# Routed experts on tokens sorted by expert, with the router moved into the batch loop

## The chip, the cores and the metric

One NeuronCore of a Trainium2 chip runs the whole program. The metric is device time in microseconds for one execution. Before the change three runs took 994.24, 994.62 and 994.80 us; the median is 994.62 us.

## What is computed

A pre-norm decoder layer on x of 16 batches x 256 tokens x 128 channels, in float32:

```
x = x + attention(layernorm(x))          # 16 heads of 8 channels, masked scores
x = x + cross_attention(layernorm(x))    # 1601 context rows per batch
x = x + ffn(layernorm(x))

ffn: scores  = softmax(x @ gate_w.T)                  # 8 experts
     indices = top_k(scores + gate_bias, 2)
     combine = one_hot(indices) * scores, summed over the 2 choices
     y = sum over e of mlp(x, w1[e], w2[e], w3[e]) * combine[:, e]
     z = mlp(x, sw1, sw2, sw3)                        # the shared expert
     mlp(x) = (silu(x @ w1.T) * (x @ w3.T)) @ w2.T    # 128 -> 256 -> 128
```

So each of the 4,096 tokens needs two of the eight experts, and the shared one.

## The kernel before

The kernel is written engine by engine: each engine has its own list of instructions in an order written out by hand, and semaphores join them. The activations stay in SBUF in `xall` (32 tiles of 128 tokens).

**The batch loop.** `batches` (L455 on) calls `step(i, nxt, new, old, crs)` on every engine for i = -1 to 17. A step works on four batches at once: it prepares batch i+1 (`nxt`: first layernorm, q and k, their split into bfloat16 parts that go through HBM and come back as `kst` and `qst`), runs the self attention of batch i (`new`: `alpha` with the row maxima, `gamma`, `p_exp`, `masked`, `values`), finishes self attention of batch i-1 (`old`: L717, L1020 to L1024, L750, L759, second layernorm, q of the cross attention and its low part `q2_lo`, L1096), and runs the cross attention of batch i-2 (`crs`: four units of `cross_scores`, `cross_max`, `cross_exp`, `cross_transposes`, `cross_values`, then L1091 adds the result to `xall`). Steps 2 to 14 are one hardware loop.

What sets the order around the change:

- TensorE (`step` from L555): `alpha(0, 1)`, then `cross_scores(0)`, which waits for `q2_lo_done` of VectorE; the matmul that makes v (L709); `alpha(1, 3)`, where `alpha(u)` waits for the row maximum of `alpha(u-2)`; L717; the sums over v (L723 to L725), which wait for `v_done`; `alpha(3, 4)` (L581); `cross_transposes(0)`; and so on to `values(3)`.
- VectorE (`step` from L943): `alpha_max(0, 1)`, `statistics` of batch i+1 (L959, L962), v (L1006), `cross_max(0)` (L984), `alpha_max(1, 2)`, den, num and rden; at the end of the step `heads_out(0)` (L1078, after the second `values`), the four adds of L1091, `q2_lo` (L1096), `heads_out(1)`.
- GpSimd: `inverse_deviation` (L1114, L1116), `on` (L1153), the two subtractions L1159 and L1161, later `info_low` (L1131: 896 and then 512 columns), `masked` (L1142), `xb` (L1206).
- SyncE issues all DMAs.

**The FFN.** `shared_step` is called with g = -4 to 7. It prepares group g+4 (4 tiles, 512 tokens: layernorm, transposes, the split of the transposed tokens into `x3_hi` and `x3_lo`, router logits) and runs the shared expert of group g. Its calls with g = -4 to -1 lie in the last step of the batch loop (`beside`), the others behind it in `rest`. A token group and one expert are one unit: `up` is 12 matmuls of 512 columns (L194: w13_hi x x_hi, w13_lo x x_hi, w13_hi x x_lo, for four blocks), Silu on ScalarE (L268), the product on VectorE (L306), `down` is 8 float32 matmuls of 128 x 128, each of which the profile shows as two (L203). The routed pass runs 8 groups x 8 experts = 64 such units, every token through every expert; VectorE adds each result into `xall`, scaled by the token's weight for that expert (L395). Router arithmetic is done once, on 128 x 256 (L324 to L347).

Of the kernel before, what the change touches and what calls it, by code (L numbers as in the profile page):

```python
# [11 lines left out]
BF16 = mybir.dt.bfloat16  # L12

# [27 lines left out]
NEG = -1.0e30  # L41
QROWS = 48
# [3 lines left out]
C_ID, C_MASK, C_U, C_ONE, C_CNT, C_BV, C_BR, C_BIAS, C_GB, C_IOTA, C_END = 0, 128, 256, 384, 512, 544, 672, 800, 804, 812, 820  # L46


def decoder_kernel(nc, x, ctx, ctxT, consts, wq, wk, wv, wr, wx, gate, w13, w2, out):
    with ExitStack() as stack:  # L50
# [10 lines left out]
        dk = nc.dram_tensor("k_stack", [HA, 6, P // HA, S], BF16).ap()  # L61

# [87 lines left out]
        def flat(b0, n):  # L150
# [4 lines left out]
        xn3, xn3T = sb("xn3", [P, GT, D]), sb("xn3T", [P, GN])  # L155
        Y_BANKS = (4, 7)
        x3_hi, x3_lo = sb("x3_hi", [P, NT * P], F32R), sb("x3_lo", [P, NT * P], F32R)
        st3, mv3, rstd3 = sb("st3", [P, GT, 6]), sb("mv3", [P, GT, 2]), sb("rstd3", [P, 2, GT])
        logit, ex, sc, biased, eq, oh1, oh2, comb = (sb(n, [P, NT, E]) for n in
                                                     ("logit", "ex", "sc", "biased", "eq", "oh1", "oh2", "comb"))  # L160
        lmax, esum, erec, m1, i1, m2, i2 = (sb(n, [P, NT]) for n in ("lmax", "esum", "erec", "m1", "i1", "m2", "i2"))
        comb_g = sb("comb_g", [P, GT, E])
        sil = [prob[z][:, 2 * GN:3 * GN] for z in range(2)]
        h = [[prob[n][:, z * GN:(z + 1) * GN] for z in range(2)] for n in range(2)]
        for n in ("ln3_stats", "ln3_aggr", "ln3_eps", "ln3_rstd", "xn3_done", "xn3T_ps", "xn3T_sb", "x3_lo_done", "lg_ps", "lg_sb",
                  "route", "ex_done", "comb_done", "comb_g_done",
                  "up_ps", "silu_done", "h_done", "y_ps", "shared_done", "acc_done"):
            s[n] = sem(n)

        def shared_step(step, g):

            step(g, g < NGR - 4, -3 <= g < NGR - 3, -2 <= g < NGR - 2, g >= 0)

        def routed_pass(eng, group):  # L180
            group(0, False)
            with eng.Fori(1, NGR) as g:
                group(g, True)

        def moe_pe(pe):
            def up(u, g, e, first=False):

                for z in range(2):
                    if not first:
                        pe.wait_ge(s["h_done"], 2 * u - 1 + z)  # L190
                    for half_w in range(2):
                        w = slice(half_w * INTER + z * P, half_w * INTER + (z + 1) * P)
                        for n, (a, b) in enumerate(((w13_hi, x3_hi), (w13_lo, x3_hi), (w13_hi, x3_lo))):
                            mm = pe.matmul(ps[:, 2 * z + half_w, :], lhsT=a[:, e, w], rhs=b[:, bass.ds(g * GN, GN)],  # L194
                                           start=(n == 0), stop=(n == 2))
                    mm.then_inc(s["up_ps"], 1)

            def down(u, e, n):

                pe.wait_ge(s["h_done"], 2 * u + 2)  # L200
                for t in range(GT):
                    for z in range(2):
                        mm = pe.matmul(ps[:, Y_BANKS[n], t * D:(t + 1) * D], lhsT=h[n][z][:, t * P:(t + 1) * P], rhs=w2_sb[:, e, z, :],  # L203
                                       start=(z == 0), stop=(z == 1))
                mm.then_inc(s["y_ps"], 1)

            def step(g, stats, norm, trans, new):
                f = g + 2
                if trans:
                    pe.wait_ge(s["xn3_done"], GT * f + GT)  # L210
                    if f:
                        pe.wait_ge(s["xn3T_sb"], 2 * f)
                    for t in range(GT):
                        mm = pe.transpose(ps[:, 5, t * P:(t + 1) * P], xn3[:, t, :], ident)
                    mm.then_inc(s["xn3T_ps"], 1)
                if new:
                    pe.wait_ge(s["x3_lo_done"], g + 1)
                    up(g, g, E, g == 0)
# [1046 lines left out]
```

## Time and profile before

| | |
|---|---|
| median of three runs | 994.62 us |
| the profiled execution: its span | 997.1 us (2.5 us over the median; no other time of it is given) |
| instructions | 19,846 |
| PE busy | 896.1 us, 90% of the span |
| DVE busy | 540.2 us, 54% |
| ACT busy | 425.3 us, 43% |
| POOL busy | 289.7 us, 29% |
| DMA | 57.49 MB, mean 58 GB/s |
| share of L194 (up) and L203 (down) in the chain that ended last | 20% and 13% |

The span has three parts. Up to about 620 us the batch loop runs, with a period of 36.0 us from step 2 on; then come the last step of the loop with the preparation of the FFN beside it, and the shared expert up to about 692 us; the rest is the routed pass. Times in the profile count from the span's start. A busy PE is not a PE at its peak, and an engine's idle time costs something only where the next engine waits for it.

### The profile page before, as it was taken

The page shows a single profiled execution, that of the slowest core. Times are in us where ns is not written, and L with a number is a line of the kernel's source. Part 1 is how long each engine was busy: PE and PEld are TensorE (multiplying, and loading weights), DVE is VectorE, ACT ScalarE, POOL GpSimd, SP SyncE. Part 2 cuts the span into 40 slices and gives each one's busy share as a digit, 9 for nine tenths or more (in the row PEclk, how much of TensorE's full clock was granted, in tenths as well). Part 3 has the DMA queues.
Part 4 walks back from the last instruction along what each step waited for, and adds up shares of the span by engine and source line. Part 5 has one row for each costly group of instructions (what it writes and reads, how often), then busy time and mean ns, then how long its engine had stood idle before and what let it go on. Part 6 is the DMA issues. An engine that isn't in the chain of part 4 may idle for free.

```text
span 997.1 us, 19846 instructions
## 1 busy us (share of the span) xinstructions
PE 896.1 (90%) x6528; PEld 694.8 (70%) x6528; DVE 540.2 (54%) x1291; ACT 425.3 (43%) x887; POOL 289.7 (29%) x495
## 2 busy tenths in 40 slices
PE   1697998998898899899899887789999999999998
PEld 0354766666676676676666666779888888888887
DVE  0443565475475465556547543556655555555554
ACT  1133555545645645555554564334222222222221
POOL 2235345435435524634633543242000000000000
PEclk9995999999999999999999999789999999999999
DMA  7124144134134224414413411000000000000000
GB/s 237 32 51 105 42 112 128 34 99 123 40 99 116 58 82 116 93 52 111 126 34 101 124 36 58 9 1 1 2 11 1 11 11 0 11 11 0 11 11 11
DMA packets 64282, 57.49 MB, mean 58 GB/s; under 512 B 5872, under 2 KB 57984, under 8 KB 64128
## 3 DMA queue, kind: packets, MB, share of 16 engines
q1 hardware_dynamic: 64256, 57.15, 21.8%
q8 instruction: 15, 0.25, 0.1%
q14 instruction: 11, 0.09, 0.0%
HBM read 45.20 MB, written 11.53 MB: 57 GB/s over the span
## 4 chain that ended last, share of the span: by engine, by line
PE 77%; ACT 5%; issue 5%; DVE 5%; POOL 3%; SPq 1%; DMA 1%; POOLq 0%; DVEq 0%; ACTq 0%
PE banks L194 20%; PE banks L203 13%; PE banks L653 7%; PE banks L610 7%; PE banks L588 4%; PE banks L636 4%; PE banks L590 3%; PE banks L691 3%; POOL prob L1142 3%; PE banks L581 2%; PE banks L583 2%; ACT prob L862 2%; DVE xmax L984 2%; PE banks L717 1%; PE banks L672 1%
## 5 line engine op out<-in xcount | busy, mean ns | idle before, releaser
L268 ACT ACTIVATE prob<-banks 128x512 f32<-128x512 f32 x144 | 86.0, 598 | 228.1 <-PE banks L194 178.7
L306 DVE TENSOR_TENSOR prob<-banks,prob 128x512 f32<-128x512 f32 x144 | 99.3, 691 | 107.0 <-ACT prob L268 106.9
L203 PEld LDWEIGHTS banks<-w_sb,prob 128*128 128x128 f32 x1152 | 139.1, 192 | 6.0
L203 PE MATMUL banks<-w_sb,prob 128*128 128x128 f32 x1152 | 140.4, 275 | 0.0
L194 PE MATMUL banks<-x_hi,w_hi 128*128 (+1 forms) x288 | 120.7, 419 | 0.1
L653 PE MATMUL banks<-info,xprobT 128*128 128x128 f32 (+1 forms) x832 | 108.3, 282 | 9.6 <-ACT xprobT L838 9.6
L976 DVE TENSOR_REDUCE mx<-banks 128x2 f32<-128x512 f32 x128 | 87.3, 683 | 50.8 <-PE banks L590 50.7
L194 PE MATMUL banks<-x_lo,w_hi 128*128 (+1 forms) x288 | 114.3, 397 | 0.0
L862 ACT ACTIVATE prob<-banks 128x512 f32<-128x512 f32 x192 | 99.8, 617 | 32.4 <-PE banks L676 32.4
L194 PE MATMUL banks<-x_hi,w_lo 128*128 (+1 forms) x288 | 113.6, 394 | 0.0
L653 PEld LDWEIGHTS banks<-info,xprobT 128*128 128x128 f32 (+1 forms) x832 | 100.0, 195 | 17.2 <-ACT xprobT L838 17.2
L826 ACT ACTIVATE xprob<-banks,xmax 128x896 f32<-128x896 f32 x64 | 59.3, 927 | 122.6 <-DVE xmax L984 122.6
L1142 POOL TENSOR_SCALAR_AFFINE_SELECT prob<-prob 128x256 f32<-128x256 f32 (+1 forms) x192 | 87.8, 482 | 34.8 <-ACT prob L862 34.5
L395 DVE SCALAR_TENSOR_TENSOR xall<-banks,comb_g,xall 128x128 f32 (+1 forms) x256 | 72.1, 344 | 34.9 <-PE banks L203 34.9
L984 DVE TENSOR_REDUCE xmax<-banks 128x1 f32<-128x896 f32 x64 | 62.5, 977 | 28.5 <-PE banks L610 19.3
L636 PE MATMUL banks<-cst,xprob 128*128 128x128 f32 (+1 forms) x416 | 58.1, 279 | 20.5 <-ACT xprob L826 20.5
L838 ACT COPY xprobT<-banks 128x512 f32<-128x512 f32 (+2 forms) x128 | 58.6, 509 | 33.6 <-PE banks L636 31.5
L636 PEld LDWEIGHTS banks<-cst,xprob 128*128 128x128 f32 (+1 forms) x416 | 48.1, 143 | 25.6 <-ACT xprob L826 24.1
L194 PEld LDWEIGHTS banks<-x_lo,w_hi 128*128 128x128 f32 x288 | 54.3, 189 | 13.4
L194 PEld LDWEIGHTS banks<-x_hi,w_lo 128*128 128x128 f32 x288 | 54.7, 190 | 10.1
L972 DVE TENSOR_REDUCE mx<-banks 128x4 f32<-128x512 f32 x64 | 43.7, 683 | 32.9 <-PE banks L583 32.8
L194 PEld LDWEIGHTS banks<-x_hi,w_hi 128*128 128x128 f32 x288 | 54.6, 190 | 9.9 <-DVE prob L306 0.3
(143 smaller groups left out, 1388.3 us busy)
## 6 DMA issues: line engine op xcount, KB each, us to landing
infoT<-in_ctxT SPq DMA_DIRECT2D x16, 800.5 KB, 5.8
info<-in_ctx SPq DMA_DIRECT2D x16, 768.0 KB
kst<-k_stack SPq DMA_DIRECT2D x32, 192.0 KB
q_parts<-parts SPq DMA_DIRECT2D x32, 96.0 KB, 2.3
k_stack<-parts SPq DMA_DIRECT2D x32, 96.0 KB, 2.3
qst<-q_parts SPq DMA_DIRECT2D x32, 96.0 KB
w_raw<-in_w SPq DMA_DIRECT2D x16, 144.0 KB, 5.5
k_stack<-parts SPq DMA_DIRECT2D x32, 64.0 KB, 2.1
```

The costliest lines, as they stand in the source:

```text
L194: mm = pe.matmul(ps[:, 2 * z + half_w, :], lhsT=a[:, e, w], rhs=b[:, bass.ds(g * GN, GN)], start=(n == 0), stop=(n == 2))
L203: mm = pe.matmul(ps[:, Y_BANKS[n], t * D:(t + 1) * D], lhsT=h[n][z][:, t * P:(t + 1) * P], rhs=w2_sb[:, e, z, :], start=(z == 0), stop=(z ...
L268: act.activation(sil[z], ps[:, 2 * z, :], ACT.Silu).then_inc(s["silu_done"], 1)
L306: dve.tensor_tensor(h[n][z], ps[:, 2 * z + 1, :], sil[z], ALU.mult).then_inc(s["h_done"], 1)
L395: dve.scalar_tensor_tensor(xt, ps[:, Y_BANKS[e % 2], t * D:(t + 1) * D].unsqueeze(1), comb_g[:, t, e:e + 1], xt, ALU.mult, ALU.add).then_i ...
L610: mm = pe.matmul(ps[:, c, 0:m1 - m0], lhsT=a[:, q], rhs=b[:, m0:m1], start=(n == 0), stop=(n == 2))
L636: mm = pe.transpose(ps[0:w, 3 + z, (m - part[0]) * P:(m - part[0] + 1) * P], xprob[hf][:, o:o + w], ident)
L653: mm = pe.matmul(ps[:, 2, u * P:(u + 1) * P], lhsT=xprobT[hf][0:w, m - blocks[0], :], rhs=info[0:w, m, :], start=(m == blocks[0]), stop=(m ...
L862: act.activation(prob[n % 2][:, kind * 512:(kind + 1) * 512], ps[:, KEY_BANKS[v % 4], :], ACT.Exp, scale=SCALE).then_inc(s["p_exp"], 1)
L976: dve.tensor_reduce(mx[:, 1, h:h + 2], bank.rearrange("p (c n) -> p c n", c=2), AX.X, ALU.max).then_inc(s["alpha_max"], 1)
L984: dve.tensor_reduce(xmax[:, u:u + 1], flat(0, HW[hf]), AX.X, ALU.max, negate=True).then_inc(s["xmax_done"], 1)
L1142: pool.affine_select(out=v, in_=v, compare_op=ALU.is_gt, fill=0.0, base=0, pattern=[[0, 4 if kind == 2 else 2], [1, P]], channel_multiplier=-1
```

## The change

`step` gets two more stages. With `rte`, batch l = i-3 is normalised, transposed and split, and its logits and its two choices are computed; with `pos`, batch o = i-4 gets the places of its rows, and the rows are sent. The loop now has steps -1 to 19, of which 4 to 14 are the hardware loop. Tokens sorted by expert lie in HBM: `sorted_rows` has a region of 4,224 rows for each expert, and a row is the 128 normalised channels, the token's weight and the row number that its result goes to (520 bytes). Each token is sent twice, by four indirect DMAs of 128 rows per batch, issued by GpSimd. Behind the loop VectorE works out the expert and the first row of each of 72 tiles (64 full ones' worth, up to 8 for the experts' rests; all 72 are always run). The FFN is then: shared groups 0 to 3; 36 pairs of sorted tiles; shared groups 4 to 7; the sum.

The core of the diff, per engine:

```diff
+TOPK = 2
+PAIRS = (B * S * TOPK // P + E) // 2
+SLOTS = 2 * PAIRS
+SB = 4
+EARLY = NGR // 2
...
-                step(-1, True, False, False, False)
...
-                with eng.Fori(2, B - 1) as i:
-                    step(i, True, True, True, True)
...
+                with eng.Fori(4, B - 1) as i:
+                    step(i, True, True, True, True, True, True)
...
+                step(B + 2, False, False, False, False, True, True)
+                step(B + 3, False, False, False, False, False, True)
```

TensorE, in a step and behind the loop:

```diff
                 cross_scores(0)
                 if old:
                     pe.wait_ge(s["oT_sb"], 2 * j + 2)
+                if pos:
+                    pe.wait_ge(s["picked"], o + 1)
+                    pe.wait_ge(s["tri_done"], 2)
+                    first = oh_bf[:, 0, :].unsqueeze(1)
+                    pe.matmul(ps[:, 7, 0:2 * E], lhsT=tri_bf[:], rhs=oh_bf[:].rearrange("p t e -> p (t e)"),
...
+                    pe.matmul(ps[:, 7, 2 * E:3 * E], lhsT=ones_bf[:], rhs=oh_bf[:, 1, :],
+                              start=False, stop=True, skip_group_check=True).then_inc(s["rank_ps"], 1)
                 if new:
...
                 cross_scores(1)
+                if rte:
+                    pe.wait_ge(s["xn3_done"], 2 * l + 2)
+                    for t in range(T):
+                        mm = pe.transpose(ps[:, 7, S + t * P:S + (t + 1) * P], xn3[:, t, :], ident)
...
                 cross_scores(3)
+                if rte:
+                    for t in range(T):
+                        mm = pe.matmul(ps[:, 7, S + t * E:S + (t + 1) * E], lhsT=xn3T[:, t * P:(t + 1) * P], rhs=gate_sb[:],
+                                       start=True, stop=True)
...
+            def experts_of(q):
+                for j in (2 * q, 2 * q + 1):
+                    expert[j] = pe.value_load(expert_i[0:1, j:j + 1], min_val=0, max_val=E)
+            def sorted_up(q):
+                for t in range(2):
+                    of = bass.ds(expert[2 * q + t], 1)
+                    for n, (a, b) in enumerate(((xT_hi, w13_hi), (xT_lo, w13_hi), (xT_hi, w13_lo))):
+                        mm = pe.matmul(ps[:, UP_BANKS[q % 2] + t, :], lhsT=a[g % 2][:, c], rhs=b[:, of, :].rearrange("p o n -> p (o n)"),
+                                       start=(n == 0), stop=(n == 2))
...
+                for g in range(EARLY):
+                    up(g)
+                    if g:
+                        down(g - 1)
+                down(EARLY - 1)
+                pe.wait_ge(s["slots_done"], 1)
+                experts_of(0)
+                sorted_x(0)
+                pe.wait_ge(s["shared_done"], EARLY)
+                for q in range(PAIRS):
+                    if q + 1 < PAIRS:
+                        experts_of(q + 1)
+                    sorted_up(q)
+                    if q % 2 == 0 and q // 2 + 1 < PAIRS // 2:
+                        sorted_x(q // 2 + 1)
+                    if q >= 1:
+                        sorted_hT(q - 1)
+                    if q >= 2:
+                        sorted_down(q - 2)
```

`sorted_x` transposes 4 tiles of sorted rows, `sorted_hT` is 4 transposes of the hidden values of a pair, `sorted_down` 4 float32 matmuls. ScalarE copies and splits (`sorted_hi`, `sorted_T`), does Silu (`sorted_silu`) and scales each tile's result by the row's weight (`sorted_y`, two per pair); VectorE does `sorted_lo` and `sorted_hid`.

VectorE in a step:

```diff
+                places()
                 alpha_max(0, 1)
+                if rte:
+                    apart(dve, "x3_done", 4 * l + 4)
+                    statistics(l, st3, mv3, "ln3_stats", "ln3_aggr")
                 if nxt:
...
                 alpha_max(2, 3)
+                if rte:
+                    normalised(l, mv3, rstd3, xn3, "ln3_rstd", "xn3_done")
...
+                route_scores()
                 heads_out(0)
+                route_choices()
                 if crs:
...
                 heads_out(1)
```

In the part left out of the last lines stand the four adds of L1091 and `q2_lo` (L1096), unchanged. `places` is 5 instructions, the first of which waits for `rank_ps`; `route_scores` is 2; `route_choices` is a chain of 18 on 128 x 16 or 128 x 32, nearly each of which waits for the one before it. Eleven of the 18 have two tensors in SBUF as inputs. In TensorE's part, the three rank matmuls have 8 to 16 columns in bfloat16.

ScalarE in a step: the copies of the transposed tokens and of the logits, the cast to `x3_hi`, and the exponential of the scores behind `p_exp(1)`.

GpSimd in a step: `inverse_deviation` of batch l at its head; the four indirect DMAs ahead of `on`; `x3_lo`, the copy of the normalised tokens into `row` (twice) and of the home numbers behind `info_low(1, ...)`, ahead of `xb`. Behind the loop 72 indirect DMAs (`sorted_home`), one for each tile's result into `routed_out`:

```diff
+                if pos:
+                    apart(pool, "placed", o + 1)
...
+                    for t in range(T):
+                        for c in range(TOPK):
+                            pool.indirect_dma_start(dsort, bass.IndirectOffsetOnAxis(ap=place[:, t, c:c + 1], axis=0), row[:, c, t, :], None,
+                                                    bounds_check=SORTED - 1, oob_is_err=False).then_inc(s["sent"], 16)
...
+                for j in range(SLOTS):
+                    sorted_home(j)
```

SyncE behind the loop: 8 register loads with two DMAs each (the pads behind each expert's rows), a wait for all rows sent, then for each of the 72 tiles a register load and a DMA of 128 rows into one of four buffers of 4 tiles (from the fifth group on after the results of the group four earlier have landed), then, once all results have landed, 16 DMAs of 256 KB that bring the two routed results of each token back. VectorE adds them to `xall` in 16 instructions of 128 x 512, and SyncE writes the output in 8 DMAs as before.

Removed: the 64 units of the routed pass, the 256 scaled adds (L395), the router arithmetic behind the loop, and the calls of `shared_step` in the last step of the loop (`beside`).

## Rows read from the trace of the kernel before

**Rows 1.** Stretches: batch loop and routed pass. us, then busy PE, PEld, DVE, ACT, POOL, clock, DMA share, GB/s
```profile
168.00:564.00 396.00, 360.74 (x3036) 259.15 (x3033) 230.01 (x518) 222.35 (x495) 182.84 (x320) 1.00 0.34 89
706.00:999.00 293.00, 286.81 (x1756) 252.49 (x1754) 160.05 (x389) 74.09 (x124) 0.00 (x0) 0.99 0.02 7
```

**Rows 2.** Chain that ended last, one unit of the routed pass: start us, us, what
```profile
977.35 2.80 PE banks L194 x12
980.15 1.78 PE banks L203 x16
```

**Rows 3.** Timeline, tail of batch step 13: start us, us, engine line op
```profile
524.63 0.69 DVE L1078 COPY oT<-banks 128x512 f32<-128x512 f32 x1 [2.11 <-PE banks L694]
...
525.77 1.38 POOL L1142 TENSOR_SCALAR_AFFINE_SELECT prob<-prob 128x512 f32<-128x512 f32 x3
...
525.98 1.25 DVE L1091 SCALAR_TENSOR_TENSOR xall<-banks,xw,xall 128x128 f32 x4 [0.66 <-POOL xw L1199]
...
527.12 1.27 POOL L1131 TENSOR_TENSOR info_lo<-infoT,info_hi 128x512 fp32r<-128x512 f32 x1
...
527.34 1.34 DVE L1096 TENSOR_TENSOR q_lo<-q,q_hi 128x256 fp32r<-128x256 f32 x1
```

**Rows 4.** Timeline, head of batch step 13
```profile
492.80 0.19 PEld L610 LDWEIGHTS banks<-info_hi,q_hi 128*128 128x128 f32 x1 [0.40 <-POOL info_lo L1131]
...
493.78 0.47 DVE L959 BATCH_NORM_STATS2 st<-xall 128x6 f32 x2
...
494.12 0.61 PE L709 MATMUL banks<-wv_sb,xn1T 128*128 128x128 f32 x4
...
494.76 0.42 DVE L1006 TENSOR_TENSOR vaug<-banks,cst 128x256 f32<-128x256 f32 x1
...
495.10 1.08 DVE L984 TENSOR_REDUCE xmax<-banks 128x1 f32<-128x896 f32 x1
...
495.63 1.04 PE L717 MATMUL banks<-cst,oT 128*128 128x128 f32 x8
...
497.27 0.39 PE L581 MATMUL banks<-kst,qst 48*128 48x128 bf16 x4
...
500.47 0.39 PE L588 MATMUL banks<-kst,qst 48*128 48x256 bf16 x2
```

**Rows 5.** All q_lo instructions (L1096): ns min/median/max, first and last start us
```profile
L1096 DVE TENSOR_TENSOR q_lo<-q,q_hi x16: 425/1336/1341, 93.7 to 620.9; 128x256 fp32r<-128x256 f32 x16
```

**Rows 6.** Timeline, DVE: a very small instruction, and two dependent ones of the router
```profile
515.44 0.16 DVE L1067 TENSOR_TENSOR xmin<-xmax 128x2 f32<-128x2 f32 x1
...
694.30 0.43 DVE L330 TENSOR_TENSOR sc<-ex,erec 128x256 f32<-128x256 f32 x1
694.76 0.42 DVE L331 TENSOR_TENSOR biased<-sc,cst 128x256 f32<-128x256 f32 x1
```

**Rows 7.** Stretches in the last batch step, as in rows 1
```profile
622.00:624.00 2.00, 0.91 (x5) 0.55 (x3) 1.05 (x2) 0.00 (x0) 0.00 (x0) 0.82 1.00 294
624.00:626.00 2.00, 0.77 (x4) 0.78 (x5) 1.20 (x9) 1.10 (x2) 0.38 (x2) 0.50 0.02 4
```

**Rows 8.** Timeline, first matmul of the shared expert
```profile
651.77 0.78 PE L194 MATMUL banks<-x_hi,w_hi 128*128 128x512 f32 x1
```

**Rows 9.** DMA: an issue on SyncE's queue (timeline), and the output's (KB, us to landing)
```profile
527.18 0.41 SPq L534 DMA_DIRECT2D info<-in_ctx  x1
...
out<-xall SPq DMA_DIRECT2D x8, 256.0 KB, 2.3
```

**Rows 10.** Costliest groups of the page, Silu: count | busy us, mean ns | idle before
```profile
L268 ACT ACTIVATE prob<-banks 128x512 f32<-128x512 f32 x144 | 86.0, 598 | 228.1 <-PE banks L194 178.7
```

**Rows 11.** Timeline, POOL: its longest instruction
```profile
517.53 2.08 POOL L1131 TENSOR_TENSOR info_lo<-infoT,info_hi 128x896 fp32r<-128x896 f32 x1
```

**Rows 12.** Timeline, DVE: an add of 128x512, and the last adds of the kernel
```profile
688.07 0.69 DVE L352 TENSOR_TENSOR xall<-banks,xall 128x512 f32<-128x512 f32 x1 [1.26 <-PE banks L203]
...
993.00 1.13 DVE L395 SCALAR_TENSOR_TENSOR xall<-banks,comb_g,xall 128x128 f32<-128x128 f32 x4 [0.66 <-PE banks L203]
```

More of the change, by code:

```diff
@@ new lines, in rest @@
+                sorted_hT(PAIRS - 1)
+                sorted_down(PAIRS - 2)
+                sorted_down(PAIRS - 1)
+                for g in range(EARLY, NGR):
+                    if g == EARLY:
+                        pe.wait_ge(s["shid_done"], PAIRS)
+                    up(g)
+                    if g == EARLY + 1:
+                        pe.wait_ge(s["sy_sb"], SLOTS)
+                    if g > EARLY:
+                        down(g - 1)
+                down(NGR - 1)
+            return rest
@@ L441, in rest, with sorted_home @@
+            return rest
+        def moe_pool(pool):
+            def sorted_home(j):
+                g = j // GT
+                pool.wait_ge(s["sy_sb"], j + 1)
+                pool.indirect_dma_start(dy, bass.IndirectOffsetOnAxis(ap=sorted_in[g % SB][:, j % GT, D + 1:D + 2].bitcast(I32), axis=0),
+                                        routed[j % 8], None, bounds_check=LAST - 1, oob_is_err=False
+                                        ).then_inc(s[f"home{j % 8}"], 16)
             def rest():
-                for g in range(NGR):
-                    shared_step(step, g)
@@ L492, in write_parts, with step @@
                                  ).then_inc(s[f"parts{a}_out"], 16)
[L494 to L495 removed]
+            def step(i, nxt, new, old, crs, rte, pos):
+                j, k, f, l, o = i - 1, i - 2, i + 1, i - 3, i - 4
                 if old and crs:
@@ L551, in _, with step @@
             pe.wait_ge(s["const_done"], 2)
-            moe_step, moe_rest = moe_pe(pe)
-            def step(i, nxt, new, old, crs):
-                j, k, f = i - 1, i - 2, i + 1
-                def beside(g):
-                    if crs and not old:
-                        shared_step(moe_step, g)
+            moe_rest = moe_pe(pe)
+            def step(i, nxt, new, old, crs, rte, pos):
+                j, k, f, l, o = i - 1, i - 2, i + 1, i - 3, i - 4
                 def alpha(u0, u1):
@@ L939, in _, with step @@
             dve.wait_ge(s["pads_done"], 2)
-            moe_step, moe_rest = moe_dve(dve)
-            def step(i, nxt, new, old, crs):
-                j, k, f = i - 1, i - 2, i + 1
-                def beside(g):
-                    if crs and not old:
-                        shared_step(moe_step, g)
+            dve.tensor_tensor(tri_bf[:], ones, upper, ALU.subtract).then_inc(s["tri_done"], 1)
+            dve.tensor_copy(ones_bf[:], ones).then_inc(s["tri_done"], 1)
+            dve.tensor_copy(filled[:], cst[:, C_REG:C_REG + E]).then_inc(s["filled_set"], 1)
+            moe_rest = moe_dve(dve)
+            def step(i, nxt, new, old, crs, rte, pos):
+                j, k, f, l, o = i - 1, i - 2, i + 1, i - 3, i - 4
                 def normalised(b, mvt, r, dst, rs, done):
@@ L1009, in step @@
                 cross_max(0)
-                if crs and not old:
-                    apart(dve, "x3_done", 4 * B - 4)
-                beside(-4)
                 alpha_max(1, 2)
```

594 lines of the change are left out of this document (352 added, 242 removed).

## The prediction, made before the changed kernel ran

> **What bounds the kernel now.** I read the stretches first, for how busy each engine is by stage; then the chain that ended last, for what TensorE's time consists of; then the timeline of one batch step, for which wait ends last; then single groups for the price of what is new.
>
> The routed pass is TensorE's: 286.8 of 293.0 us busy [rows 1], and its chain is a strict alternation of 12 up matmuls in 2.80 us and 16 records of down in 1.78 us [rows 2]. A unit is 4.58 us, an up matmul 0.233 us, a float32 matmul of 128 x 128 0.22 us. 64 units are 293 us. From the shared expert's first matmul at 651.8 [rows 8] to the span's end are 345.3 us.
>
> The batch loop is also mostly TensorE's (360.7 of 396.0 us [rows 1]), but a step's seam hangs on VectorE. At the tail, heads_out(0) starts at 524.63, the four adds of L1091 run from 525.98 to 527.23, q2_lo from 527.34 to 528.68 [rows 3], and the next step's cross_scores(0), one period of 36.0 us after the one at 492.80 [rows 4], starts at 528.8. So whatever VectorE gets between heads_out(0) and q2_lo beyond its present pause there moves the whole next step. The change puts its longest new chain there.
>
> Sums are made against the profiled span, 997.1 us, which is 2.5 us over the median of the runs; I subtract that at the end. A measurement can tell about 0.2% (2 us) from no change.
>
> **Routed experts, the gain.** A pair of sorted tiles has 6 up matmuls (6 x 0.233 = 1.40 us [rows 2]), 4 transposes of hidden values and 2 of rows (8 take 1.04 us [rows 4], so 6 x 0.13 = 0.78), and 4 down matmuls (0.89 [rows 2]): 3.07 us. ScalarE has less: Silu 0.60 [rows 10], and three more pieces of at most that size. What no row shows is the register load, two per pair on TensorE and one per tile on SyncE. Below, it costs nothing, if the matmuls issued ahead of it still run; above, I bound it by a DMA's landing, 2.3 us [rows 9]. A load reads one number and moves no tile, so it is nearer to an issue, 0.41 us [rows 9]; I take 0.5 us, of which 0.12 us survives on TensorE, 0.23 us per pair. A pair is then 3.3 us, 36 pairs 119 us, and 3 us for filling and draining the pipeline: 122 us. The ends are 3.07 us (111 us) and 3.07 + 4.6 = 7.7 us (276 us).
>
> **GpSimd's scatter.** 72 indirect DMAs, two per pair. They are hidden as long as one costs less than 1.65 us of GpSimd. Nearest rows: a DMA's issue on SyncE, 0.41 us [rows 9], and GpSimd's longest instruction, 2.08 us [rows 11]. It has 128 row numbers to take in, which a plain issue hasn't, so I take the middle, 1.3 us: hidden, with 0.35 us to spare. The Trainium skill ("DMA: Bandwidth & Descriptors", Latency and other measured facts) gives about 1 us to a first byte on GpSimd's path, by which the sum would be the same; no run here shows it yet.
>
> **The seam of a step.** route_choices is 18 dependent instructions. A tiny one takes 0.16 us and the gap between dependent ones is 0.03 us [rows 6]; with 0.18 us for 16 to 32 elements the chain is 3.8 us. But 11 of the 18 have two SBUF inputs, and q2_lo, of that kind, shows what happens beside GpSimd: alone it takes 0.425 us, beside L1131 1.336 us [rows 5], ending 0.29 us after GpSimd does [rows 3]. Behind heads_out(0) GpSimd is busy nearly without a pause: masks 1.38, info_low 1.27 [rows 3], then the new x3_lo (half of L1131's 512 columns, 0.65), row copies (about 0.7) and xb: some 4.8 us. Ends: no blocking but for q2_lo, 3.8 us; each such instruction waiting out one of GpSimd's, 3.8 + 4.2 = 8.0 us. I take 7.0, nearer the upper, because the row that shows it is of the same kind. The new tail is 525.32 + 7.0 + 1.27 + 0.45 + 0.1 = 534.1 against 528.8: **+5.3 us** a step (ends +2.1 and +6.3). route_scores lies in VectorE's pause before heads_out(0) (2.11 us [rows 3]) and costs nothing; without that pause it would cost 0.4.
>
> That blocking is stated as a rule in the Trainium skill ("SBUF — State Buffer", SBUF: two separate sides): VectorE's two-SBUF-input instructions and GpSimd's take a shared port pair in turn, each for its whole length. It speaks against this change; taken for all of GpSimd's instructions it gives the upper end, 8.0, and the trace bears it out for L1131 and q2_lo only.
>
> **The head of a step.** places() is now first on VectorE and waits for the rank matmuls, which follow cross_scores(0): they end where v began, 1.32 us after 492.80 [rows 4], plus 0.3. Behind it queue alpha_max(0), then the extra statistics (0.98 us, from 493.78 to v's add at 494.76), the old ones, v's add and cross_max(0) (1.0 us pitch) [rows 4]. With 1.05 us for places' five, alpha_max(0) ends at +3.4, v's add at +5.7 and alpha_max(1) at +7.3. TensorE's L581 needs the last: at +7.4 instead of +4.5 [rows 4]. Then cross_scores(1), two new transposes (0.27) and the next alpha at +11.45, where L588 stood at +7.67 [rows 4]: **+3.8 us** (ends 2.5 and 4.5). From there TensorE leads again; the new logits (4 records, about 0.5) and ScalarE's copies add **+0.7**. The four indirect DMAs stand ahead of `on`, whose reader is some 8 us off; at 1.3 us each they are covered, above 2.5 us not.
>
> **The clock.** TensorE now idles about 5 us at each seam. In the last step of before, 0.91 us of work in 2 us was followed by a granted clock of 0.50 of full, the 1.2 GHz level [rows 7]. Half speed in the head is mostly under VectorE's chain; I take **+1.0 us** (ends 0 and 3).
>
> A full step costs 5.3 + 3.8 + 0.7 + 1.0 = **10.8 us**, 12 of them (steps 4 to 15) 130 us. Step 3 lacks places: +7. Step 16: +8. The last cross step loses beside() but gains the same chains; then batch 15's normalisation, router and ranks run one after the other across four engines, about 10 us with TensorE idle: from 621.4 [rows 5] the first shared matmul comes after 36.7 us instead of 30.4, +6. Together 151 us: 651.8 becomes 803.
>
> **Behind the loop.** Four shared groups at 4.58 us, and the slot arithmetic (12 small instructions, 4.5 us) ahead of their products: 21.6 us. Meanwhile SyncE, free 5.3 us in, does 8 x (0.5 + 2 x 0.43), a landing of 2.3, 4 x 0.93 and another 2.3: with waits 25.6 us, and the first rows' split adds 1.6 more: 27.2 us. Routed: 122. The rest: last results landed +5.7 us; 4 MB back in 16 DMAs at 200 to 294 GB/s [rows 7], 14 to 20 us, under the four shared groups (20.5 us); then 16 adds of 0.69 [rows 12], one after the other, 11; then as now 3.0 us from the last adds (until 994.1 [rows 12]) to the end: 34.5. Sum: 803 + 27.2 + 122 + 34.5 = 986.7, so 10.4 us less than 997.1: **984.2 us** against 994.6. Behind the loop 345.3 become 183.7, a gain of 161.6, and 151 of it are lost in front.
>
> **The rivals.**
> - *VectorE isn't blocked* (chain 3.8 us, no clock loss): a step costs 2.1 + 3.8 + 0.7 = 6.6, 4.2 less, 12 of them 50 us less: **934 us**. For it: only one pair of instructions shows blocking, and the masks are short. Chance 0.24.
> - *Blocked in full* (8.0 us, as the rule above has it): 12 us more and 2 at the edges: **998 us**, no gain. For it: all of GpSimd's work there reads SBUF. Chance 0.15.
> - *The routed stage isn't TensorE's*, the slower side: GpSimd's indirect DMA, in `sorted_home`. At 2.3 us a pair is 4.6 instead of 3.3: +47, **1031 us**; it decides from 1.65 us on, and from 1.8 us on nothing is left of the gain. A register load of 1.2 us on TensorE would do the same. For it: no row prices either. Chance 0.19.
> - *Most of the new waits are absorbed*: a step costs 3.5, 7.3 less, 88 us in all: **896 us**. Against it: TensorE idles 35 us in 396 [rows 1], so there is little to absorb. Chance 0.06.
> - All 72 tiles run whatever the routing is, so the data can't undo the saving; that the operand picked by a register slows a matmul is within the rival of the routed stage, and the routed pass already had such operands.
>
> **How the numbers follow.** The forecast has 0.36; its own range is 964 to 1004, and two thirds of it lie over 2 us below 994.6. Faster: 0.36 x 0.65 + 0.24 + 0.15 x 0.25 + 0.19 x 0.05 + 0.06 = 0.58. Within 0.2%: 0.06. Slower: 0.36. The range takes in both neighbours and half of the slow case: 925 to 1035.
>
> **What would show it.** A period of the loop of 46 to 48 us (43 without blocking), with TensorE's longest wait before cross_scores(0), released by q_lo; the chain from heads_out(0) to q_lo 7 us longer; two-input router instructions of 0.2 to 1.4 us instead of 0.18; a granted clock of 0.5 at each seam; pairs of 3.3 us with TensorE over 90% busy; SyncE's loads before the first pair as the longest wait behind the loop. The prediction is wrong if the period stays under 42, or if pairs take over 4 us.

## The result, and the profile after

The changed kernel takes 1008.1 us (median of 4 runs, 1007.9 to 1012.6) beside 994.7 us for the kernel before: ratio 1.0143, 95% interval 1.0122 to 1.0164. It is slower by 1.4%; 984.2 us, faster, was predicted. The profiled execution has a span of 1006.0 us against 997.1, so the comparison of the two traces has 8.9 of the 13.4 us to explain.

**The batch loop.** The same stretches as [rows 1], of the changed kernel: the loop (its ten middle periods), then the new routed stage.

```profile
217.00:672.00 455.00, 361.68 (x2830) 260.82 (x2850) 275.44 (x782) 208.63 (x490) 228.21 (x380) 0.91 0.29 76
820.00:972.00 152.00, 121.56 (x708) 103.53 (x708) 36.20 (x54) 69.92 (x157) 64.97 (x67) 0.91 0.20 58
```

TensorE was busy for 91% of the loop before and is now for 79%; its clock is 0.91 of full. In the routed stage it is busy for 80%. The routed pass before stood at 98%.

The timeline of the changed kernel, with the tail of one step and the head of the next, is to be laid beside [rows 3] and [rows 4]:

```profile
481.45 0.69 DVE L1240 COPY oT<-banks 128x512 f32<-128x512 f32 x1 [1.67 <-PE banks L764]
482.06 0.16 DVE L1127 TENSOR_REDUCE esum<-ex 128x2 f32<-128x16 f32 x1
...
484.26 1.28 POOL L1296 TENSOR_TENSOR info_lo<-infoT,info_hi 128x512 fp32r<-128x512 f32 x1
...
484.42 1.16 DVE L1132 SCALAR_TENSOR_TENSOR biased<-oh,biased 128x16 f32<-128x16 f32 x1
...
488.34 0.19 DVE L1140 TENSOR_REDUCE row<-ohw 128x4 f32<-128x32 f32 x1 [0.25 <-DVE ohw L1137]
488.70 1.25 DVE L1255 SCALAR_TENSOR_TENSOR xall<-banks,xw,xall 128x128 f32 x4 [0.17 <-DVE row L1140]
489.87 0.41 DVE L1260 TENSOR_TENSOR q_lo<-q,q_hi 128x256 fp32r<-128x256 f32 x1
...
490.43 0.79 PE L678 MATMUL banks<-info_hi,q_hi 128*128 128x512 f32 x1 [4.20 <-DVE q_lo L1260]
...
493.16 0.17 DVE L1147 TENSOR_TENSOR rank<-banks,filled 128x16 f32<-128x16 f32 x1 [2.27 <-PE banks L785]
...
498.27 0.39 PE L649 MATMUL banks<-kst,qst 48*128 48x128 bf16 x4 [0.66 <-DVE mx L1074]
...
501.70 0.39 PE L656 MATMUL banks<-kst,qst 48*128 48x256 bf16 x2
```

From heads_out(0) (L1240) to the next cross_scores(0) (L678) are 8.98 us; before, 4.17. This stretch is called the seam below, and the one behind it the head. In between lies the router's chain, 6.47 us from esum to the end of row. From cross_scores(0) to the last of the three alphas are 11.27 us instead of 7.67. The one wait that is new and long on TensorE is the one ahead of L678, released by q_lo.

**The routed stage.** Waits of TensorE in it, and the chain that ended last through one turn, from the load of rows to the load of rows two groups on:

```profile
PE banks L252 <- DMA infoT<-sorted_rows: 22.5, 9, 4.7
PE banks L281 <- ACT oT L364: 4.2, 5, 2.5
```

```profile
880.58 1.12 PE banks L252 x4
881.70 0.85 PE banks L281 x4
882.55 1.63 PE banks L292 x8
884.21 0.38 ACT vaug L372
...
885.35 0.98 POOL routed_out L479
...
888.07 0.98 POOL routed_out L479
...
889.35 2.24 DMA routed_out<-vaug,infoT
...
891.68 0.28 SPq L605
...
892.40 0.33 SPq L606
...
896.27 0.70 SPq L606
897.00 0.89 DMA infoT<-sorted_rows
```

The last of the group's four scatters, which the chain counts as a DMA, stands in the timeline of GpSimd:

```profile
889.35 0.98 POOL L479 DMA_INDIRECT routed_out<-vaug,infoT  x1 [0.30 <-issue]
```

TensorE transposes a group's rows (L252), goes on to the down products of the pair before the last (L292), ScalarE scales them, and GpSimd scatters four tiles. The last scatter has landed 2.24 us after its start, and only then may SyncE read four registers and load four tiles over the buffers that the scatters had as their source of indices. The next L252 of this chain starts at 898.15: 17.5 us for two groups, four pairs. Other turns are shorter: at 4.17 us a pair (run 1 has its rows) the mean turn is 16.7 us.

By stage (starts of the first or last instruction of each, predicted values behind): first shared matmul 790.3 us (803); from there to the first routed one 29.9 us (27.2); routed stage, up to the last down product at 972.9, 152.8 us (122); rest 33.1 us (34.5).

### The profile page after: what moved, and what is told of

It is laid out like the page before. It is cut to its first block, busy times and chain, and to the rows that moved or that the text cites. A ratio compares the mean times of both kernels' runs of the same rounds, so it can differ in the third digit from the quotient of the medians.

```text
span 1006.0 us, 19059 instructions
## 1 busy us (share of the span) xinstructions
PE 755.9 (75%) x5473; PEld 563.1 (56%) x5504; DVE 509.4 (51%) x1357; ACT 421.2 (42%) x966; POOL 440.3 (44%) x690
## 4 chain that ended last, share of the span: by engine, by line
PE 41%; DVE 23%; issue 13%; ACT 7%; SPq 5%; DMA 4%; POOL 3%; another core or an unknown queue 2%; DVEq 1%; ACTq 0%; POOLq 0%
PE banks L678 8%; PE banks L721 6%; PE banks L704 3%; DVE xmax L1082 3%; PE banks L656 3%; ACT prob L950 3%; PE banks L658 2%; PE banks L761 2%; POOL routed_out L479 2%; DVE biased L1132 2%; SPq L605 2%; PE banks L292 1%; DVE eq L1112 1%; PE banks L270 1%
## 5 line engine op out<-in xcount | busy, mean ns | idle before, releaser
L950 ACT ACTIVATE prob<-banks 128x512 f32<-128x512 f32 x192 | 98.6, 607 | 32.3 <-PE banks L744 32.3
L1307 POOL TENSOR_SCALAR_AFFINE_SELECT prob<-prob 128x256 f32<-128x256 f32 (+1 forms) x192 | 87.8, 485 | 38.7 <-ACT prob L950 38.6
L678 PE MATMUL banks<-info_hi,q_hi 128*128 128x512 f32 (+1 forms) x96 | 49.1, 512 | 69.0 <-DVE q_lo L1260 67.5
L479 POOL DMA_INDIRECT routed_out<-vaug,infoT x56 | 54.7, 977 | 100.1 <-ACT vaug L372 85.1
L1322 POOL DMA_INDIRECT sorted_rows<-row,place x64 | 64.9, 1014 | 25.1 <-issue 25.1
L446 DVE TENSOR_TENSOR xprobT<-banks,xprob 128x512 f32<-128x512 f32 x36 | 24.9, 692 | 90.6 <-ACT xprob L358 73.4
L678 PEld LDWEIGHTS banks<-info_hi,q_hi 128*128 128x128 f32 x96 | 22.1, 231 | 71.8 <-issue 50.0
L761 PE MATMUL banks<-prob,vaug 128*32 128x256 f32 x512 | 45.7, 430 | 20.6 <-POOL prob L1307 17.9
L1333 POOL TENSOR_TENSOR qk_r<-qk,parts 128x512 f32<-128x512 f32 x16 | 18.5, 1158 | 96.9 <-ACT parts L940 96.9
L1070 DVE TENSOR_REDUCE mx<-banks 128x4 f32<-128x512 f32 x64 | 43.9, 685 | 27.7 <-PE banks L651 23.6
L1296 POOL TENSOR_TENSOR info_lo<-infoT,info_hi 128x896 fp32r<-128x896 f32 (+1 forms) x32 | 53.8, 1680 | 2.2 <-ACT info_hi L1000 1.3
L656 PE MATMUL banks<-kst,qst 48*128 48x256 bf16 x256 | 53.0, 290 | 1.7 <-DVE mx L1070 1.1
```

What stands on the lines that cost most here:

```text
L479: pool.indirect_dma_start(dy, bass.IndirectOffsetOnAxis(ap=sorted_in[g % SB][:, j % GT, D + 1:D + 2].bitcast(I32), axis=0), routed[j % 8], ...
L656: pe.matmul(bank[:, c * S:(c + 1) * S], lhsT=qst[r, g, P:S], rhs=kst[r, g, :], start=(c == 0), stop=False, skip_group_check=True)
L678: mm = pe.matmul(ps[:, c, 0:m1 - m0], lhsT=a[:, q], rhs=b[:, m0:m1], start=(n == 0), stop=(n == 2))
L761: pe.matmul(o[32 * c:32 * c + 32, :], lhsT=vaug[:, 0, 4 * n + c, :], rhs=prob[n % 2][:, c * S:(c + 1) * S], start=True, stop=False, skip_g ...
L950: act.activation(prob[n % 2][:, kind * 512:(kind + 1) * 512], ps[:, KEY_BANKS[v % 4], :], ACT.Exp, scale=SCALE).then_inc(s["p_exp"], 1)
L1307: pool.affine_select(out=v, in_=v, compare_op=ALU.is_gt, fill=0.0, base=0, pattern=[[0, 4 if kind == 2 else 2], [1, P]], channel_multiplier=-1
```

## The experiments

Two theories stood after this. **Theory R**: the routed stage is set by the ring of four input buffers. **Theory S**: in the loop, what counts is that the router's chain stands where the next step waits for it, although VectorE has an idle stretch of 5.87 us (473.3 to 479.2) shortly before. The rivals are named with each run. Where a run has no interval it is one execution, and only distances inside its trace count: up to the first shared matmul, traces with one and the same loop differ by 6 us (789.0 with six buffers in run 1, 795.2 in run 5).

**1. Six buffers.**

```
-SB = 4
+SB = 6
...
-        sorted_in.append(info[...][:, 0:GT * ROW]...)
+        sorted_in += [info[...][:, n * GT * ROW:(n + 1) * GT * ROW]... for n in range(SB - 3)]
... (and a semaphore for each further group)
```

> Edit: the ring of input buffers of the routed stage has six groups instead of four (three on infoT, three on info), nothing else. Theory R (the ring's latency sets the pair): in the trace of the changed kernel the load of group g+4 waits for the home scatters of group g, and the loop L252 -> y -> scatters -> landing -> four register loads and loads -> L252 takes 17.5 us and comes round once in two groups, so a pair costs 4.24 us. With six buffers the same loop has four groups to come round in, 17.5 / 8 = 2.2 us a pair, under the 3.2 to 3.4 us that PE and the DVE/ACT hand-overs need: the routed stage goes from 152.8 to 115 to 122 us, the kernel to about 975 us (970 to 980). Rival I (issue: SP's register loads and POOL's 1.28 us a scatter set the pair): neither is changed, pair stays at 4.2 us, kernel 1004 to 1010. Rival P (PE's value loads and half speed): the same, 1004 to 1010.

980.3 us beside 993.5 for the kernel before, ratio 0.9875 (0.9816 to 0.9934): this one change turns the loss into a gain. The span is 978.3 us, 27.7 less. The row of the up matmuls (ns min/median/max, then the start of the first and of the last) spans 35 pairs and one tile; the quotients below take it for 35 pairs, in every run alike.

```profile
L271 PE MATMUL banks<-w_hi,info_hi x72: 392/473/787, 816.3 to 939.3; 128*128 x72
```

123.0 / 35 = 3.51 us a pair; the changed kernel (820.2 to 966.0) has 4.17. The wait of L252 for its rows is gone from the waits; the longest left on TensorE in the stage are

```profile
PE banks L282 <- ACT oT L365: 5.9, 7, 1.7
PE banks L271 <- DVE xprobT L447: 4.5, 7, 0.8
```

The mechanism held and the gain was a little smaller than forecast: the kernel takes 980.3 us (970 to 980 expected), the stage 129.0 us, not 115 to 122 (the other 3.9 us of the span's gain lie ahead of the stage, which starts at 816.3 instead of 820.2). TensorE is busy 113.7 of 129 us there, 3.16 us a pair. With four buffers it was busy 122.4 us in the same stage: some 8 of the 23.8 us that the stage lost are matmuls that ran slower beside the waits, at a granted clock of 0.91 instead of 0.98.

**2. Three buffers.** The same constant, 3.

> Edit: the ring has three groups instead of four. Theory R: the loop of 17.5 us has one group to come round in, so a group of two pairs costs about 17 us, 17 groups 290 to 300 us against 152.8, kernel about 1145 us (1120 to 1160). Rival I and rival P: the pair is set by issue or by PE, one buffer less costs little, kernel under 1030.

The kernel takes 1132.9 us. The up matmuls, and the longest of TensorE's waits, are:

```profile
L270 PE MATMUL banks<-w_hi,info_hi x72: 392/476/791, 817.8 to 1092.6; 128*128 x72
```

```profile
PE banks L252 <- DMA infoT<-sorted_rows: 140.1, 15, 10.2
```

A pair takes 7.85 us, a group 15.7: the loop comes round once in one group instead of once in two. GpSimd's scatters (0.98 us), SyncE's loads and TensorE's register loads (0.30 us) are the same in number and price, so the rivals I and P fall.

**3. Five buffers.** The same constant, 5.

> Edit: the ring has five groups. Theory R: the loop of 17.5 us has three groups to come round in, 17.5 / 6 = 2.9 us a pair, under the 3.5 us that TensorE needs there (six groups gave 3.51); so five groups do already what six did: pair 3.5 to 3.6 us, kernel 975 to 985. If instead the scatters' landing grows with the number in flight, or a group more of slack is worth something each time, the pair lies halfway between 4.17 and 3.51: 3.8 us, kernel about 992.

It takes 988.4 us in its one execution, 3 us above the expected range. The up matmuls are:

```profile
L271 PE MATMUL banks<-w_hi,info_hi x72: 392/476/792, 821.9 to 943.2; 128*128 x72
```

121.3 / 35 = 3.47 us, as with six. The higher total lies outside this row: the stage starts 5.6 us later than with six, and from the last up matmul to the last down product are 9.3 us instead of 6.0. That end isn't peculiar to five buffers: it is 9.8 us in run 4, with four, and 8.0 us in run 5, with six. Its cause stays open.

**4. Four buffers, a shorter loop.**

```
-                if g >= SB:
-                    for j in range(GT * (g - SB), GT * (g - SB + 1)):
-                        sp.wait_ge(s[f"home{j % 8}"], 16 * (j // 8 + 1))
                 for t in range(GT):
                     j = GT * g + t
+                    if g >= SB:
+                        n = j - GT * SB
+                        sp.wait_ge(s[f"home{n % 8}"], 16 * (n // 8 + 1))
```

> Edit: the ring keeps its four groups, but SyncE waits per tile for the one scatter that frees its place, ahead of that tile's load, instead of for the group's four scatters ahead of the first. Theory R: of the loop of 17.5 us, the three register loads and loads of 1.1 us that stand in line behind the last scatter's landing drop out, since they now run while the scatters (1.28 us apart) still land: 14.2 us for two groups, 3.55 us a pair, about what TensorE needs (3.51): the pair goes from 4.17 to 3.5 to 3.65 us, kernel 18 to 23 us under the changed one, about 987 us, without any more memory. Rival (what the two further buffers gave was room for something else than this latency): the pair stays near 4.2.

The kernel takes 986.0 us beside 993.8, ratio 0.9905 (0.9874 to 0.9936). The pair is 122.7 / 35 = 3.51 us by the up matmuls, and of TensorE's wait for rows little is left:

```profile
L270 PE MATMUL banks<-w_hi,info_hi x72: 392/474/790, 819.3 to 942.0; 128*128 x72
```

```profile
PE banks L252 <- DMA infoT<-sorted_rows: 3.9, 4, 2.1
```

So the wait is latency in a loop of dependent work, and either remedy removes it: more buffers, or fewer loads in line behind the last scatter.

**5. Register loads off TensorE.** With the ring of six, the expert of a tile is a constant (tile number modulo 8) and not a register; the routed output is then that of other experts than the router chose.

```
-                    expert[j] = pe.value_load(expert_i[0:1, j:j + 1], ...)
+                    expert[j] = j % E
```

> Edit: ring of six, and the experts of the sorted tiles are constants of the program (tile number modulo 8) instead of registers that TensorE loads; with it the routed output is that of wrong experts, all sizes and transfers stay. It prices the register loads on TensorE, two per pair, which the prediction put at 0.23 us per pair. By that a pair falls from 3.51 us to about 3.3. If loads are wholly hidden: 3.5 still. If they cost what a load costs on SyncE (0.42 us each, in line): 2.8, where GpSimd's 2.56 us for two scatters is next.

```profile
L271 PE MATMUL banks<-w_hi,info_hi x72: 392/476/776, 825.0 to 942.6; 128*128 128x512 f32 x72
```

A pair takes 3.36 us against 3.51. Other runs without the ring's wait have 3.46 (run 9) to 3.51 (runs 1 and 4), so two register loads cost TensorE 0.10 to 0.15 us, by one execution. The prediction had 0.23.

**6. The router's chain in VectorE's pause.** The routed stage is untouched.

```
 (VectorE)
                 if old:
                     normalised(j, mv2, rstd2, xn2, "ln2_rstd", "xn2_done")
+                route_scores()
+                route_choices()
...
-                route_scores()
                 heads_out(0)
-                route_choices()
 (ScalarE: the exp into ex moves from behind p_exp(1) to ahead of p_exp(0))
```

> Edit: on DVE the router's scores and choices stand right behind the normalised xn2 (where DVE was idle for 5.87 us, up to the reciprocal of xden), on ACT the router's exp stands ahead of the first exp of the probabilities. The first shared-expert path is untouched. Theory S (the router's chain of 20 small operations at the step's end is what delays the next step's first cross scores: 8.98 us from heads_out(0) to L678, against 4.17 in the kernel before): the chain of 6.5 us moves into the idle stretch, the seam falls to 4.2 to 4.9 us, the loop period from 45.5 to 41.0 to 41.5 us, kernel 1008 - 13 x 4.3 = about 952 us (945 to 965). Rival C (the chain is only moved: it now delays xrec, the weights xw and the last masks on POOL, and what was an idle stretch was shared with POOL, so that the operations stretch): the period falls by under 2 us, kernel 985 to 1010.

The kernel takes 920.2 us, ratio 0.9277 (0.9232 to 0.9322): 88 us less than the changed kernel, where theory S gave 56. The period is 39.06 us (L1087 from 230.31 to 581.88, nine periods) instead of 45.49, a gain of 6.43 us a step where 4 to 4.5 were expected. Tail and head:

```profile
430.58 0.17 DVE L1127 TENSOR_REDUCE esum<-ex 128x2 f32<-128x16 f32 x1 [1.55 <-ACT ex L1012]
...
435.85 0.19 DVE L1140 TENSOR_REDUCE row<-ohw 128x4 f32<-128x32 f32 x1 [0.25 <-DVE ohw L1137]
436.07 0.17 DVE L1237 RECIPROCAL xrec<-xden 128x2 f32<-128x2 f32 x1
436.85 0.69 DVE L1242 COPY oT<-banks 128x512 f32<-128x512 f32 x1 [0.61 <-PE banks L764]
...
439.55 1.34 DVE L1260 TENSOR_TENSOR q_lo<-q,q_hi 128x256 fp32r<-128x256 f32 x1
...
441.03 0.49 PE L678 MATMUL banks<-info_hi,q_hi 128*128 128x512 f32 x1
...
447.71 0.39 PE L649 MATMUL banks<-kst,qst 48*128 48x128 bf16 x4 [0.66 <-DVE mx L1074]
```

The seam is back at 4.18 us, 4.80 less, and TensorE waits for nothing ahead of L678. Rival C falls: xrec comes at 436.07, and heads_out(0) still waits for TensorE. The head is 1.16 us shorter as well (6.68 us from L678 to L649 instead of 7.84), though nothing was moved there. Two stretches of each trace (columns as in [rows 1]) say why: first the seam, then the head, of the changed kernel,

```profile
485.00:490.00 5.00, 1.22 (x16) 0.67 (x9) 4.19 (x14) 0.00 (x0) 2.60 (x5) 0.50 1.03 280
490.00:494.00 4.00, 3.57 (x13) 2.88 (x13) 1.62 (x7) 0.00 (x0) 0.00 (x0) 0.50 0.27 103
```

and of this one:

```profile
436.00:441.00 5.00, 3.90 (x61) 2.09 (x61) 3.56 (x9) 3.52 (x8) 4.54 (x9) 1.00 0.58 112
441.00:445.00 4.00, 3.43 (x23) 2.43 (x24) 2.63 (x12) 0.00 (x0) 1.86 (x4) 1.00 1.11 302
```

Behind a seam in which TensorE worked 1.22 of 5 us, the granted clock is 0.50, the 1.2 GHz level, and cross_scores(0) takes 2.40 us up to the rank matmuls (490.43 to 492.83). Behind a seam with 3.90 of 5 us the clock is 1.00, the 2.4 GHz level, and the same six matmuls take 1.31 us (441.03 to 442.34). Seam and head together are 5.96 of the 6.43 us; the other 0.47 lie later in the step. Twelve steps make 77 of the 93.6 us by which the span is shorter (912.4 instead of 1006.0); the routed stage has 4 more of them (148.2 us) though nothing was changed in it.

**7. GpSimd's copies away from the chain.** Against the changed kernel, x3_lo and the copies into row move to ahead of the deviation of ln2, where GpSimd was idle for 4.0 us.

```
+                (the block "if rte: ... x3_lo ... row ... home")
                 if old:
                     inverse_deviation(j, mv2, ...)
...
                 info_low(1, slice(H0, MF3))
-                (the block)
```

> Edit: against the changed kernel, only GpSimd's x3_lo (0.71 us), the copy into row (0.61) and the copy of home (0.18) stand in its pause ahead of the deviation of ln2, not beside the second half of the router's chain. Theory B (VectorE's two-input operations take turns with GpSimd's work): the chain from esum to the last reduce, 6.5 us, loses what these three stretch, some 1.0 us (L1111, L1112 and L1114 of the second choice, 0.45, 0.52 and 0.58, nearer to 0.17); the period goes from 45.5 to 44.3 to 44.8. Rival N (the stretched durations are no matter of GpSimd, say PSUM or ScalarE's traffic): chain and durations as before, 6.5 us; the period is 45.5.

It takes 995.8 us in its one execution. The chain takes 5.71 us (479.10 to 484.81) instead of 6.47, the seam 8.22 instead of 8.98, and the period is 44.88 us instead of 45.49 (44.3 to 44.8 expected). The second choice, of the changed kernel and then of this run:

```profile
486.29 0.52 DVE L1112 TENSOR_TENSOR eq<-eq,cst 128x16 f32<-128x16 f32 x1
486.85 0.17 DVE L1113 TENSOR_REDUCE ind<-eq 128x2 f32<-128x16 f32 x1
487.05 0.58 DVE L1114 TENSOR_TENSOR oh<-cst,ind 128x16 f32<-128x16 f32 x1
```

```profile
482.64 0.17 DVE L1110 TENSOR_REDUCE best<-biased 128x2 f32<-128x16 f32 x1
482.85 0.45 DVE L1111 TENSOR_TENSOR eq<-biased,best 128x16 f32<-128x16 f32 x1
483.33 0.18 DVE L1112 TENSOR_TENSOR eq<-eq,cst 128x16 f32<-128x16 f32 x1
483.54 0.17 DVE L1113 TENSOR_REDUCE ind<-eq 128x2 f32<-128x16 f32 x1
483.74 0.17 DVE L1114 TENSOR_TENSOR oh<-cst,ind 128x16 f32<-128x16 f32 x1
```

GpSimd's last instruction there (xb) now ends at 483.27; from then on the operations take 0.17 to 0.18 us. Theory B holds: in this chain only operations with two SBUF inputs are stretched, and only beside GpSimd's work. The gain is 0.76 us, not 1.0.

**8. The places later in the head.** `alpha_max(0, 1)` and both statistics ahead of `places()`.

```
-                places()
                 alpha_max(0, 1)
...
                     statistics(f, st, mv, "ln1_stats", "ln1_aggr")
+                places()
```

> Edit: on DVE the five operations of the places (rank, filled, ohr, place_f, place) stand behind the first alpha maximum and both statistics, ahead of the bias of v, instead of first in the step. Theory H (DVE idles 2.27 us ahead of rank, since it waits there for PE's rank matmuls behind the first cross scores, and what is queued behind it comes late): alpha(3), L649, comes 1.8 us earlier after the first cross scores (7.84 to about 6.0), period 45.5 to 43.7, kernel 1008 - 12 x 1.8 = about 986 (982 to 994). Rival (the head is set by PE at half clock or by the chain through xmax and ACT): under 0.5 us a step, kernel 1002 to 1008.

The kernel takes 992.6 us, ratio 0.9980 (0.9956 to 1.0004) to the kernel before: level with it, 15.5 us less than the changed one. The trace is that of the slowest of its ten executions (999.2 us). In it the period isn't one number: 43.3 and 45.3 us alternate. The mean of eight is 44.33 us, 1.2 less than 45.49 rather than 1.8. Two neighbouring steps, first a short and then a long one:

```profile
444.29 0.79 PE L678 MATMUL banks<-info_hi,q_hi 128*128 128x512 f32 x1 [3.67 <-DVE q_lo L1260]
...
450.89 0.39 PE L649 MATMUL banks<-kst,qst 48*128 48x128 bf16 x4
...
487.64 0.79 PE L678 MATMUL banks<-info_hi,q_hi 128*128 128x512 f32 x1 [4.55 <-DVE q_lo L1260]
...
496.04 0.60 PE L649 MATMUL banks<-kst,qst 48*128 48x128 bf16 x4
```

L649 stands 6.60 us behind L678 in the one and 8.40 in the other. Up to 3.7 us behind L678 both run at a granted clock of 0.50. In the next 4 us it is 0.91 in the short step and still 0.50 in the long one, with TensorE busy for all of both. So theory H holds where full speed comes back in time, and the gain there is 2.1 us a step; elsewhere the clock takes it all. What decides which of the two happens, the traces don't show.

**9. All three.** Runs 1, 6 and 8 together.

> Edit: the three changes together: six input buffers, the router's choices in VectorE's pause, the places behind the statistics. If they act in different stages, the sum of what each gave holds: the ring alone took 28 us off the span, the router's move 94, the places 9 to 15 (less here, since TensorE is back at full speed in the head and leads there again): about 875 us (865 to 885), faster than both kernels. If router's move and head order give the same idle time twice, 885 to 895. A pair stays at 3.5 us.

The kernel takes 883.1 us beside 994.0, ratio 0.8886 (0.8871 to 0.8901). The period is 37.8 us, in all steps alike to 0.2 us, and 1.8 us are left over the 36.0 of the kernel before. This is 125 us less than the changed kernel and 11% less time than the kernel before.

**10. All three, and GpSimd's copies as in run 7.**

> Edit: e5_all, and GpSimd's x3_lo and the copies into row stand in its pause ahead of the deviation of ln2 instead of at the step's end. Theory B (two-input operations of VectorE are stretched by GpSimd's work beside them): q_lo, 1.34 us beside these copies after the router's move, goes back to 0.41; but TensorE's alpha(0) ends within 0.1 us of it, so a step gains 0.1 to 0.5 us, kernel 2 to 6 us under e5_all. Without such a coupling q_lo keeps its 1.34 us and nothing is gained.

The kernel takes 887.6 us, ratio 0.8912 (0.8887 to 0.8938). The interval overlaps that of run 9, so it isn't shown to be slower, but the 2 to 6 us that were expected aren't there. The expectation was a miss: q_lo keeps its 1.33 us (434.90 to 436.24), since what stands beside it is info_low(1) (434.68 to 435.96), which was not moved. The period is 37.96 us against 37.77; why it is 0.2 us longer stays open.

**11. All three, and five shared groups ahead.** EARLY = 5 instead of 4.

> Edit: e5_all with five shared groups ahead of the routed stage and three behind instead of four and four. Theory W (ahead of the routed stage TensorE stands 5.8 us for SyncE's pads and first loads, and behind it the back loads, issued from 7 us after the stage's end on and landing over 12 us, set the end with the last adds): ahead 4.6 us of work fill the pause and the stage starts at the same time; behind, one group less leaves the adds waiting for the back loads instead of for the groups: 0 to 4.6 us gained, kernel 2 to 5 us under e5_all. Rival: the tail is set by the back loads and adds alone and the front by TensorE: 4.6 us slower ahead, nothing gained behind, so 1 us faster to 4 us slower.

The kernel takes 881.2 us, ratio 0.8867 (0.8839 to 0.8895), against 0.8886 of run 9: the intervals overlap, so no difference can be told.

## Why the prediction was wrong

**The step that failed** is the price of a pair, "A pair is then 3.3 us, 36 pairs 119 us". The measured pair is 4.17 us, and "pairs take over 4 us" was among the prediction's own signs of being wrong. The price was put together from instructions and from the busiest engine, and the ring of four buffers didn't appear in it. The buffers' release hangs on the landing of a scatter: 16.7 us in the mean (17.5 in the turn shown) from one L252 to the one two groups on, where four pairs without the wait take 14.0. Run 1 shows that this alone turned the forecast's sign: with it removed the kernel is faster than before, by 1.2%. It isn't the largest cost: the seam is, as run 6 shows, but the seam had been forecast. Of the stage's excess of 30.8 us (152.8 against 122) the ring made 23.8 (152.8 to 129.0 in run 1); the other 7 are the pair of 3.51 us without the ring's wait (3.3 priced). Of it TensorE is busy for 3.16 (3.07 priced); the profile doesn't count register loads as busy, so their 0.10 to 0.15 us lie in the rest, beside the hand-overs to ScalarE and VectorE at which TensorE stands.

The rival of the slower side had the right stage and sign and the wrong cause. GpSimd's scatter takes 0.98 us and 0.30 to the next, where 1.3 in all was predicted. As a rate that is hidden, as predicted: two scatters are 2.56 us of a pair's 4.17, about 60%. As latency it isn't, since the scatters stand in the loop that frees the buffers. An engine can be far from busy and still set the pace as part of a loop. The register loads were a little cheaper than priced.

**Point by point.**
- *Seam*: predicted +5.3 us a step, measured +4.8. Blocking was right in kind (run 7) and a little less in amount: the chain has 6.47 us, 7.0 was taken. The durations over 0.16 to 0.19 us sum to 2.6 us; the rest, 3.9, is the unblocked chain (3.8 predicted). The first rival (no blocking) and the second (in full) were both wrong. The rule of the Trainium skill ("SBUF — State Buffer", SBUF: two separate sides) gives the shared port pair to one of the two for its whole instruction and blocks the other until then. The trace agrees: L1132 takes 1.16 us and ends 0.04 us behind L1296, beside which it started. Most others met only the end of one of GpSimd's instructions and lost 0.15 to 0.4 us, which is why the upper end was not reached.
- *Head*: predicted +3.8, measured +3.6 at the third alpha, though not as worked out: rank came 2.73 us behind L678, predicted 1.6, because of the half clock, and the queue behind it was shorter than priced.
- *New work and clock*: predicted +0.7 and +1.0; period 45.49 less 36.0 is 9.5, so 1.1 remains for what the head doesn't already hold. Run 6 puts the half clock at about 1.1 to 1.2 us in the head: the seam and the clock are one cost, and whoever closes the seam gets both back.
- *Front*: first shared matmul at 790.3, not 803: 12 steps x 1.3 us are 15.6 of the difference, and the steps around them cost 3 us more than priced.
- *Start of the routed stage*: 29.9 instead of 27.2. SyncE needs 1.6 us for each of the eight pads (1.36 priced), and TensorE stood 5.8 us for the first rows.
- *Tail*: 33.1 instead of 34.5.

The front was 12.7 us better than predicted and the back 32 worse. Without the ring's wait the span would have been 982.2 us where 986.7 was predicted, and the kernel's time 984.3, next to the 984.2 predicted. That closeness is luck: 12.7 us too much in front and 8.3 too little behind nearly cancel. The bound for slower (1031) held the result; its weight, 0.19, was too small for a stage none of whose waits a row of before could show.

## What to carry to other kernels

Price a pipelined stage twice: by its busiest engine, and by each loop that frees a buffer, as the latency round the loop (results, scatter, landing, wait, register reads, load, landing) divided by the work that the buffers let run ahead. Here 17.5 us gave 8.75, 4.4 and 2.9 us a pair for three, four and five buffers; measured were 7.85, 4.17 and 3.47, the last being what the engines need. Where a store reads its indices from the input buffer, that buffer is held to the end of the store; wait for it piece by piece. Before a chain of small operations goes to the end of a loop's step, look for the engine's idle stretch earlier in the step: moving the same 20 instructions there took 6.4 us off each step.

## What was not expected of the hardware

- The half clock is passed on: closing 4.8 us of seam gave 6.4 us a step, since the next 3 to 4 us of TensorE had run at 1.2 GHz (0.79 and 0.63 us a matmul of L678 instead of 0.49 and 0.39). In run 8 the slow stretch lasted some 9 us in every other step, though TensorE was busy throughout its second half, and that cost 2 us more.
- A VectorE operation of 128 x 16 elements took 1.16 us beside one of GpSimd's, against 0.17 alone; GpSimd's masking with one input (L1307) stretches VectorE's as well, by 0.15 to 0.25 us.
- A scatter of 128 rows keeps GpSimd busy for 0.98 us, the next starts 0.30 us later, and the last of a group has landed 2.24 us after its start. A register read on SyncE, with the load that uses it, takes 1.1 to 1.5 us in the chain shown, of which the read is 0.28.
